# A table for the steps of the softmax maxima in a fused transformer kernel

## What is computed

```python
def layer(h, p):                      # six times
    scores = jnp.einsum('bhqd,bhkd->bhqk', q, k) * scale    # 16 heads of 8 columns
    scores = scores * smask                                 # smask[i, j] = ((i & j) == 0)
    a = jax.nn.softmax(scores, axis=-1)
    att = jnp.einsum('bhqk,bhkd->bhqd', a, v) ... @ wo + bo_
    h = _ln(h + att, g1, be1)                               # norm 0
    ff = jax.nn.gelu(h @ w1 + b1_, approximate=False) @ w2 + b2_
    h = _ln(h + ff, g2, be2)                                # norm 1
    return (h, None)
```

## Time and profile before

| | us |
|---|---|
| median of 3 runs | 1638.24 |
| lowest, highest | 1637.89, 1642.91 |
| profiled execution | 1639.42 |
| its span | 1637.60 |

### The profile page before, as it was taken

How to read it: one execution, slowest core, us unless ns; L and a number is a source line. 1 busy time by engine, 2 the same in 40 slices (tenths; PEclk the granted TensorE clock), 3 DMA queues, 4 the chain that set the end, 5 groups by cost and what they waited for, 6 DMA issues and landing times.

```text
span 1637.6 us, 63841 instructions
## 1 busy us (share of the span) xinstructions
PE 1312.1 (80%) x28552; PEld 695.8 (42%) x28552; DVE 929.2 (57%) x1929; ACT 894.2 (55%) x1555; POOL 351.5 (21%) x567
## 2 busy tenths in 40 slices
PE   2679898889888888888997998988888887585833
PEld 1345555545554545455554545544433333131311
DVE  3564555655455555545556555455577577687356
ACT  1256666566665666666665666655455654253610
POOL 3122222222222222122222112223011110101021
PEclk7699999999999999999999999999999999798976
DMA  8443234423442442333344334423221231100000
GB/s 162 89 106 76 76 86 90 105 65 63 84 103 70 93 92 71 81 72 86 77 90 105 73 54 84 104 73 86 34 70 25 67 70 44 30 2 3 9 7 7
DMA packets 133894, 114.06 MB, mean 70 GB/s; under 512 B 42368, under 2 KB 121054, under 8 KB 133214
## 3 DMA queue, kind: packets, MB, share of 16 engines
q1 hardware_dynamic: 133622, 109.99, 30.6%
HBM read 62.69 MB, written 47.25 MB: 67 GB/s over the span
## 4 chain that ended last, share of the span: by engine, by line
PE 34%; issue 26%; DVE 24%; POOL 7%; ACT 5%; DMA 2%; SPq 1%; POOLq 0%; DVEq 0%; ACTq 0%
PE pD L711 14%; DVE MX L1110 8%; PE pV L781 7%; PE pT L711 6%; PE pS L728 6%; DVE DEN L1302 4%; DVE X L1232 2%; PE pD L880 2%; ACT PT L1013 2%; POOL RS L1421 2%; DVE YE L1224 1%; DVE R L1320 1%; DVE CC L1162 1%; DVE DEN L1295 1%; ACT SQ L1028 1%
## 5 line engine op out<-in xcount | busy, mean ns | idle before, releaser
L1013 ACT ACTIVATE PT<-pT 128x512 f32<-128x512 f32 x1120 | 640.0, 596 | 559.5 <-PE pT L711 501.4
L1110 DVE TENSOR_REDUCE MX<-pS 128x1 f32<-128x512 f32 (+4 forms) x928 | 501.0, 573 | 504.4 <-PE pS L728 500.5
L711 PE MATMUL pT<-Qop,Kop 128*32 128x256 bf16 (+2 forms) x7168 | 452.8, 305 | 31.3 <-ACT PT L1013 17.7
L728 PE MATMUL pS<-Kop,Qop 128*32 128x128 bf16 (+4 forms) x7168 | 318.3, 262 | 81.4 <-DVE MX L1110 52.9
L781 PE MATMUL pV<-PT,Vp 128*32 128x256 f32 (+2 forms) x3584 | 315.3, 440 | 0.7 <-ACT PT L1013 0.7
L728 PEld LDWEIGHTS pS<-Kop,Qop 128*32 128x32 bf16 x7168 | 177.7, 99 | 266.0 <-issue 126.3
L711 PEld LDWEIGHTS pT<-Qop,Kop 128*32 128x32 bf16 x7168 | 187.6, 97 | 182.5 <-issue 88.6
L1421 POOL TENSOR_TENSOR RS<-VAR,MHALF 128x4 f32<-128x4 f32 x60 | 60.7, 1012 | 443.2 <-DVE VAR L1169 443.2
L781 PEld LDWEIGHTS pV<-PT,Vp 128*32 128x32 f32 x3584 | 122.4, 111 | 71.4 <-issue 24.8
L711 PE MATMUL pD<-H1T,W 128*32 128x512 f32 x768 | 99.8, 605 | 26.0 <-ACT HIDT L1084 24.1
L1455 POOL TENSOR_TENSOR ATT<-NUM,DEN 128x512 f32<-128x512 f32 x28 | 35.8, 1279 | 389.3 <-DVE DEN L1302 389.3
(11 more groups left out here) (146 smaller groups left out, 1277.5 us busy)
## 6 DMA issues: line engine op xcount, KB each, us to landing
Qop<-Qs SPq DMA_DIRECT2D x56, 384.0 KB
Kop<-Ks SPq DMA_DIRECT2D x56, 384.0 KB
Qs<-XS SPq DMA_DIRECT2D x28, 384.0 KB, 2.6
Ks<-XS SPq DMA_DIRECT2D x28, 384.0 KB, 3.1
Qs<-XS SPq DMA_DIRECT2D x28, 256.0 KB, 2.9
Ks<-XS SPq DMA_DIRECT2D x28, 256.0 KB, 3.1
EM<-Es SPq DMA_DIRECT2D x24, 256.0 KB, 3.2
Ms<-MROW SPq DMA_DIRECT2D x336, 4.0 KB, 1.5
```

Source lines behind the costliest of these rows:

```text
L711: ins = matmul(dst[c:min(c + 32, cols)], lhs[:, c:min(c + 32, cols)], rhs, start=start, stop=stop, tile_position=(0, c))
L728: ins = matmul(pS[32 * c:32 * c + 32, k % 2, at:at + w], Qop[:, it.par, h, R * qb:R * (qb + 1)], Kop[:, it.par, h, :] if qb == 0 or it.ful ...
L1013: ac.activation(dst, pT[:, k % 2, :], ACT.Exp, scale=SCALE).then_inc(t_used, 1)
L1110: ins = ve.tensor_reduce(MX[:, u, g2, qbs[0]:qbs[-1] + 1:step], pS[:, k % 2, at:at + w * len(qbs)].rearrange("p (h n) -> p h n", n=w), axi ...
```

## The change

step_maxima gets a table for masked items. Unit k of a masked item stands in step MAX_STEPS[k]: units 0 to 4 in steps 0 to 4, units 5 to 10 in steps 7 to 12, units 11 to 21 in steps 20, 21, 22, 22, 23, 24, 24, 25, 26, 26, 27. No unit stands in steps 5, 6, 13 to 19 and 28 to 35. Full items keep the even spread. The order of the units, the instructions, the buffers and the waits stay as they are; what changes is where the units stand in the lists of TensorE and VectorE. The lists of ScalarE, GpSimd and SyncE don't change.

```diff
--- before.py
+++ after.py
@@ -49,6 +49,7 @@
 
 PIECES = {1: [0], 2: [1, 2], 3: [3]}
 WP_STEPS = (15, 17)
+MAX_STEPS = (0, 1, 2, 3, 4, 7, 8, 9, 10, 11, 12, 20, 21, 22, 22, 23, 24, 24, 25, 26, 26, 27)
 WP_TILES = ((0, 1), (2, 3))
 WP_SUMS = ((9, None), (7, 4), (6, 5), (0, 8))
 W1_STEPS = (22, 23, 24, 24)
@@ -545,6 +546,8 @@
         def step_maxima(it, step):
 
             n = it.max_units()
+            if not it.full:
+                return [k for k in range(n) if MAX_STEPS[k] == step]
             return range((step * n + STEPS - 1) // STEPS, ((step + 1) * n + STEPS - 1) // STEPS)
 
         block = ctx.enter_context(nc.Block())
```

## The result

The change makes the kernel slower: 1657.99 us in the median of 13 runs (1652.35 to 1668.93) against 1645.73 for the kernel before, run beside it (13 runs, 1637.03 to 1654.93). The ratio is 1.0083, with an interval of 1.0057 to 1.0109. The kernel before is 7.5 us higher over its 13 runs than over the 3 shown, and that alone puts the median outside: the ratio, laid on 1638.24, gives 1651.8, inside the range but outside the forecast's own case of 1638 to 1646. The change costs 12.3 us between the medians, where I had 4.

The account below looks back on a forecast made before the run. TensorE, busy 80%, was taken as the bound, its idle time movable. Turns 11 x 0.22 - 6 x 0.33 + 5 x 0.1 = +0.9, start +2.5: +3.4, rounded to +4; about 1643.4 profiled, forecast 1642, range 1630 to 1655.

Parts of the forecast that it names:

- the forecast's own case of 1638 to 1646: Whole kernel: time lands near the 1642 forecast; chance 0.42, of which 0.27 within 0.3% and 0.15 above.
- One sign: Stage 1, step 14: a stall of about 1 us before the CM matmul, put down to R.
- the sum's term for stage 3: RB0 to W1_2: unit 11 heads VectorE's queue in step 20, delaying NUM and V; +1.5 a turn, bounds +1.2 and +1.8.
- the ordinary turn: Slot-loop turn with masked items, 11 of 22 full turns: six stage terms summing to +0.22 us each.
- The five turns at the V projection: Turns whose first item is at the V projection: one more column waits, stage 3 loses 1.4; +0.1 a turn.
- Stage 1 of a layer's first turn: Exp 0 to VAR0 in 6 turns: unit 9 no longer runs at half clock; about -0.45, the turn -0.33.
- The start: Two slots before the first full turn: shift rows leave VectorE later, behind more units, delaying exp 0; +2.5 us.
- Rival 1: Step 20's queue costs full price: stage 3 loses 1.8, with +0.4 in stage 1 1655, alone 1648; chance 0.24.
- Rival 2: Norms' gain in stages 2 and 5 wins through slack in R or exp 23 not gating W1_2; 1632, chance 0.22.
- Rival 3: Nothing moves: the turn is held by shift-row transfers or ScalarE's exponentials; 1638, chance 0.08.
- Rival 4: TensorE's clock falls after stalls of 1.0 to 1.1 us three times a turn; 1679, chance 0.04.
- The page that spoke against the change: Skill's rule that interleaving regimes may help; the table sets stages further apart, so slower throughout; no size given.

Follow-up runs that it names:

- e0: The changed kernel run again unaltered for a second profile; 1658.74 us, ratio 1.0098 to the kernel before.
- e5: The kernel before with its even steps written as a table, so the same lists; ratio 0.9998 to the kernel before.
- e4: Even spread of the kernel before with seven units moved one to two steps, none directly ahead of a chain's link on VectorE; 1623.86 us, ratio 0.9871 to it.
- e3: The changed kernel with unit 11 in step 21 instead of step 20; 1637.43 us, ratio 0.9975 to the kernel before.
- e1: Front half of the change alone: units 0 to 10 by the table, units 11 to 21 in their even steps; 1653.05 us, ratio 1.0066 to the kernel before.
- e8: Kernel before with only the early units moved: units 2 to 4 in steps 2, 3, 4 instead of 3, 4, 6; ratio 0.9987 to it.
- e9: Kernel before with only units 5 to 10 moved, to steps 7 to 12 as in the change, the rest even; ratio 1.0057 to it.
- e6: The changed kernel with half of the Q and K head rows transferred (24 of 48); ratio 0.9915 to the kernel before.
- e7: The kernel before (even steps) with half of the Q and K head rows transferred (24 of 48); ratio 0.9868 to the unaltered kernel before.

## Why the prediction was wrong

**The positions were right.** R starts 14.59 after exp 0 where it started 14.20 (forecast 0.46 later), and CM 15.39 where it started 15.00 (forecast 0.44 later), again 0.15 after R ends:

```profile
840.87 0.65 DVE L1323 SCALAR_TENSOR_TENSOR R<-pD,BQK,XS 128x512 f32<-128x512 f32 x1
```

VAR0 comes 0.06 later (forecast 0.1). RB0 and RB1 follow their variances by 1.81 and 1.86 (1.81 and 1.82). V stands 2.77 behind RB0 (2.74), W1_2 8.67 (8.74). One sign was wrong: no stall of 1 us stands before CM. TensorE comes late to it itself, after a wait of 0.25 for a copy by ScalarE (841.18), so that no idle is left that R would end. TensorE's waits for R grew by 4.2 us in all, from 7 waits to 17.

**The step that failed is the sum's term for stage 3, +1.5 a turn.** I had 8.74 for after, and set it against 7.25, a mean over turns of which several held an idle of the fetch kind; with the claim that new stalls would hide those, the price became 1.5. The floor of the stage before is 6.90, the floor after is 8.67, and the price is 1.77. Over all 22 turns the stage grew by 45.7 us, 2.08 a turn: 1.81 without the idles in it, and the rest because these idles went from 4.7 to 10.6 us instead of hiding. With 1.77 the ordinary turn is 0.48 and not 0.22: 11 turns, 2.9 us more. The five turns at the V projection go by the same: 7.51 (two turns; the others 7.82 to 8.60) became 9.29 (one 9.47), which is 1.78 and not 1.4, so 0.48 a turn instead of 0.1 and 1.9 us more. Stage 1 of a layer's first turn was to gain 0.45. Without the idles it was 25.66, 24.89, 25.31, 26.23 and 26.15 before and 25.86, 25.50, 24.83, 25.06 and 25.54 after, 0.29 less in the mean; in e0 the mean is 25.63, and in e5, with the order of before, 25.55, so I can't show a gain there; without it 2 us more.

**The start was too dear.** Exp 0 still waits for the shift rows, 2.56 (69.39) and 0.92 (105.35), but VAR0 of the first full turn is 1.53 late (130.81 against 129.28), not 2.5:

```profile
69.39 0.62 PE L714 MATMUL pT<-Qop,Kop 128*32 128x512 bf16 x4 [2.56 <-DMA Qop<-Ms]
105.35 0.40 PE L714 MATMUL pT<-Qop,Kop 128*32 128x512 bf16 x4 [0.92 <-DMA Qop<-Ms]
```

The sum with these terms is 3.4 + 2.9 + 1.9 + 2.0 - 1.0 = 9.2, without the growth of the idles.

**The idles did not shrink, they grew.** This is the assumption behind the failed term and it missed in its own right: 7.8 us more. Together that is 17.0, against 14.7 in the spans (the start's 1.5 and the 7.8 share 1.0 us of idles). The two timelines, added up stage by stage, close the account: without idles the 22 turns are 8.5 us longer (stage 3 by 39.8; stages 1, 2, 4, 5 and 6 shorter by 2.4, 9.4, 2.1, 16.8 and 0.5) and the start 0.5, the idles are 7.8 longer (1.0 of it in the start, 6.7 in the turns), and behind the last masked turn the changed kernel makes up 2.1, most of it before VAR0 of the first turn with a full item. What makes that turn shorter isn't shown. Most of the growth falls late. VAR0 is 5.4 later than before at 1087.18, and 15.3 later at 1216.47; between stand these three, and two smaller ones (0.91, 1.37), where the kernel before has 1.26 and 1.09:

```profile
1096.54 0.20 PE L731 MATMUL pS<-Kop,Qop 128*32 128x64 bf16 x1 [1.79 <-issue]
1124.36 0.73 PE L714 MATMUL pD<-IDF,RS 128*32 128x128 f32 x17 [2.69 <-issue]
1160.13 0.40 PE L714 MATMUL pT<-Qop,Kop 128*32 128x256 bf16 x8 [3.17 <-issue]
```

**The rivals.** Rival 1 was the true one. Its first half, stage 3 at 1.8, is what was measured (1.77), and its 1648 lacks only the idles. Its second half, 0.4 more in stage 1, did not happen (0.06). That its price of 1655 lies near the profiled 1654 is luck: the idles filled the place of that half. Rival 2 fell: there was no slack in R's chain, exp 23 did gate W1_2. Rival 3 fell: the turn moved by 0.48 with the places of the maxima, and e4 shows with its 1.3% that it can also get shorter. Rival 4 fell: with 23 stalls for NUM of up to 1.3 us the granted clock stayed at 1.00, its full level of 2.4 GHz, in all six stages, and is 0.98 in the mean over the masked part of either kernel (66 to 1190 us before, 66 to 1210 after). What the Trainium skill tells of short idles between groups of matmuls (TensorE: Matmul & The Clock Gate, A second HAM failure mode: psum-queue depth-cycling) is not seen in this trace.

**The page that spoke against the change.** The Trainium skill (Perfetto Trace Analysis, Optimization Strategy) gave the sign for the change as a whole, 1.0083. But by that rule the crowded order would be the slower one throughout, and it isn't: e3 leaves the rear crowded, moves one unit by a step, and has a ratio of 0.9975. Crowding cost 0.99 a turn in stage 3 and gave 1.34 back elsewhere; what turned the sum was the 0.78 of one reduction directly ahead of a chain's link on an in-order queue. e4 (0.9871) says the same, for it moves seven units by one or two steps off such places and is about as evenly spread as the kernel before.

**What stays open.** Why the front placement raises the fetch idles: e1, e8 and e9 show that it does, and e6 and e7 that they need the transfers for the larger part. What TensorE waits for in them can be read from the traces, as told under the last heading; how the order of the maxima makes more of these waits isn't followed.

## What to carry to other kernels

When work is moved out of the way of one chain, look at what stands directly behind its new place on the same in-order queue; a reduction in front of a link that others wait for cost 0.78 us in each turn here, more than its own length, and one step later it cost nothing. Price a stage against its floor over the turns, not against a mean that holds idles, and don't let two unknowns hide each other without a row that shows it. A gain in the stages isn't yet a gain in the span: e4 earned 27 us by its stages and kept 14.

## What the runs showed of the hardware

TensorE's idles without a releaser are 7 to 28 us of a run here, and for the most part they belong to the program: the same instructions have them in repeats, and the order of the maxima, with the same instructions in number, moves their sum between 12 and 28 us (front even and nothing else moved: 13.1 and 13.4; front by the table: 20.9, 20.5, 22, 23.3).

What TensorE waits for in them shows when their places and the DMA packets are laid side by side. First, the places. Count TensorE's matmuls from the first one: all 233 such idles of the thirteen profiles stand at numbers that are 126.69 or a multiple of it apart, to within two matmuls, whatever the order of the maxima and whatever the matmul there does. Second, the packets. Beside q1, which carries the kernel's own transfers, a queue q8 of the kind "instruction" moves 225 packets of 16384 bytes in each run, one for every 127 of the 28552 matmuls, and each of the 233 idles ends 1.2 to 1.9 us after one of them has landed. So TensorE waits there for the next part of its own list. Third, the load. Of the 32 idles of the kernel before and the changed one, 30 have q1 at over 0.7 of the 16 engines in the 2 us before the packet starts (0.95 in the mean); of the other 404 packets of these two runs (the first and last few left out), 113 have it (0.35 in the mean). So the packet is late beside the large transfers, and half the transfers (e6, e7) leave half the idles.

The DMA answer for the stretch of the idle before 469.57, and for that before 1124.36, both of the changed kernel:

```profile
q1 hardware_dynamic: 398, 0.40, 97.9%
```

```profile
q1 hardware_dynamic: 1, 0.00, 0.0%
```

The first idle (2.63) stands while the queue fills 97.9% of the 16 engines, the second (2.69) while it moves nothing. That looks as if the load had no part in the second, but the packet must be looked at, not the idle. The windows 1119.5 to 1121.5 and 1121.5 to 1121.7 show q1 until the packet starts, and the packet itself:

```profile
q1 hardware_dynamic: 205, 0.22, 82.9%
```

```profile
q8 instruction: 1, 0.02, 47.3%
```

47.3% of 16 engines over 0.2 us is 1.51 us for the one packet, which lands at 1123.11; the matmul starts at 1124.36. For the first idle the same two windows are 464.3 to 466.3 and 466.3 to 466.5:

```profile
q1 hardware_dynamic: 368, 0.37, 87.5%
```

```profile
q8 instruction: 1, 0.02, 50.0%
```

That packet takes 1.60 us and lands at 467.96, and the matmul starts at 469.57.
